# The end of a mixture-of-experts stage, its last block and its pooled sums, and the order of the first loads

## The chip, the cores and the metric

The kernel runs on one core of a Trainium2 chip. TensorE (PE in the profile), VectorE (DVE), ScalarE (ACT), GpSimd (POOL) and SyncE (SP) run their own instruction streams, joined by semaphores. The metric is device time in microseconds; the median of 3 runs is 857.94 (857.0 to 859.44).

## The reference

A macaron block on x of shape (4, 512, 256), float32:

```python
x = x + 0.5 * ffn(layernorm(x))
x = x + attention(layernorm(x))        # lightning attention, 16 heads, chunks of 128
x = x + 0.5 * ffn(layernorm(x))        # the same weights

def ffn(x):                            # 12 experts, top 3
    probs = softmax(x @ Wr + br); top_vals, top_idx = top_k(probs, 3)
    ew = softmax(top_vals); out = 0
    for e in range(12):
        sel = top_idx == e             # tokens that chose e
        w_e = sum(where(sel, ew, 0)) / max(sel.sum(), 1)      # one weight per expert
        h = relu(x @ w1[e] + b1[e]) @ w2[e] + b2[e]           # 256 -> 640 -> 256
        out = out + sel.any(-1) * (w_e * h)
    pooled = out.mean(axis=1)          # one row per batch
    phi = sigmoid(relu(pooled @ Wp1 + bp1) @ Wp2 + bp2)
    return out * (1 - 0.8 * (phi > 0.7))
```

## The kernel before, in words

The program calls the ffn stage twice (f = 0 and 1, "call 0" and "call 1") with attention between. The 2048 tokens are 16 tiles of 128, four chunks of positions (`NC`) by four batches (`B`). Each call has three parts.

*Routing* normalises the tokens, stores them as rows in DRAM (`xn_rows`), computes the router and builds a table that sorts the 6144 token-expert pairs into 35 blocks of 256 (`NB`), each block one expert's.

*Blocks.* For each block POOL gathers its 256 rows by two indirect DMAs, PE transposes them (L816), multiplies by `w1` (`first`, L824: 30 matmuls), ACT applies relu (L695), DVE splits the result into a high and a low half-precision part (L1321, L1323), PE multiplies by `w2` (`second`, L840: 30 matmuls), DVE weighs it and adds b2 (`weigh`, L1331), and POOL adds the rows to an accumulator in DRAM by two indirect DMAs (`scatter`, L510). Even blocks go to accumulator 0, odd ones to accumulator 1 (`LANES`). PE interleaves three blocks: transposes of block b + 2, `first` of b + 1, `second` of b. On POOL gather b + 4 stands ahead of scatter b. In call 0 the weights are split into two half-precision parts for one expert per block in the first dozen blocks (L583, L1112), which lengthens those blocks.

*Combine.* SP waits for all scatters (L470) and loads both accumulators, chunk by chunk, into `O` and `O2` (L474); DVE adds them (L1390); PE sums every batch over its tokens with a column of ones, 32 float matmuls (L905); DVE scales (L1392), PE and ACT compute phi from two small products, DVE turns it into a factor, and updates x by `O` times the factor (L1407). In call 1 SP writes each batch of x out after its update (L480).

All orders are written out by hand; each engine runs its own program, and semaphore waits set the rest. SP issues in program order: inputs, weights, zeros for the two accumulators of call 0 (L429, `clear_sums`), b2 broadcast to all partitions (L465), attention weights and the zeros of call 1 between blocks, accumulators, output. POOL's first scatter of a call waits for the zeros; its first gathers wait for the table. b2 is multiplied by the experts' weights on ACT in call 0 (L681), on POOL in call 1 (L524).

In the profile L759 is the helper through which all matmuls are recorded, so one line stands for many; a float32 matmul is recorded as two instructions.

## Time and profile before

| | us |
|---|---|
| median of 3 runs | 857.94 |
| profiled execution, whole | 856.17 |
| its span, first to last instruction | 854.4 |
| PE busy | 693.0 (81%) |
| DVE busy | 530.5 (62%) |
| POOL busy | 429.3 (50%) |
| ACT busy | 310.4 (36%) |

The span falls into a start of some 60 us, 35 blocks of call 0 until about 340, its combine until about 370, attention until about 515, routing of call 1 until 555, 35 blocks until 815, and the last combine until the end. PE's busy share is near full in the blocks and low in both combines. Busy time counts an engine's instructions; the granted clock of PE, given beside it in the windows, says at which speed they ran (1.00 is 2.4 GHz, 0.50 is 1.2 GHz).

### The profile page before, as it was taken

Reading aid. Unit: us, or ns where it says so; the run is one execution under the profiler, and the core shown is the slowest. Engines: PE = TensorE matmul, PEld = TensorE weight load, DVE = VectorE, ACT = ScalarE, POOL = GpSimd, SP = SyncE. Lnnn points to the kernel's source line nnn. Section 1 sums busy time; section 2 is a strip of 40 time slices with the busy share of each in tenths; the row PEclk is TensorE's granted clock in tenths of the full one; section 3 lists DMA queues with packets and bytes.
Section 4 is the critical chain, followed back from the end, with each engine's and each line's share of the span. In section 5 each row is a group of like instructions: output and inputs, shape, how many; then the busy total and the mean of one; then the engine's idle time right before and its main releaser. Section 6 shows DMA issues by size and latency. Waiting matters only on the chain. (4 is left out here: it accounts for less than half of the span.)

```text
span 854.4 us, 20887 instructions
## 1 busy us (share of the span) xinstructions
PE 693.0 (81%) x6526; PEld 602.8 (71%) x6527; DVE 530.5 (62%) x1066; ACT 310.4 (36%) x692; POOL 429.3 (50%) x304
## 2 busy tenths in 40 slices
PE   1415999899999996659999984169999999999834
PEld 1314777788889985657777773159999999999734
DVE  6894998745555553268888879935555555555413
ACT  3785866433333331023222212323333333333200
POOL 0014488888888875010101000076888888888520
PEclk9756999999999999569999995579999999999965
DMA  9998144655555554610000003033444444444373
GB/s 307 377 365 283 30 72 62 148 93 112 95 111 92 111 93 62 204 49 3 0 0 0 1 2 99 18 112 57 76 77 74 74 75 76 76 74 74 50 196 123
DMA packets 76739, 85.51 MB, mean 100 GB/s; under 512 B 6944, under 2 KB 68384, under 8 KB 76320
## 3 DMA queue, kind: packets, MB, share of 16 engines
q0 software_dynamic: 26880, 36.72, 26.2%
q1 hardware_dynamic: 49824, 48.35, 17.0%
q8 instruction: 19, 0.31, 0.2%
q14 instruction: 16, 0.13, 0.1%
HBM read 50.97 MB, written 34.08 MB: 100 GB/s over the span
## 5 line engine op out<-in xcount | busy, mean ns | idle before, releaser
L759 PE MATMUL PS<-W,A 128*128 (+1 forms) x2228 | 275.1, 279 | 14.1 <-DVE A L1452 7.5
L759 PE MATMUL PS<-A,W 128*128 128x256 f16 (+1 forms) x2356 | 278.5, 277 | 4.3 <-issue 2.8
L510 POOL DMA_INDIRECT expert_sums<-A,place x140 | 233.6, 1668 | 75.0 <-issue 39.3
L495 POOL DMA_INDIRECT A<-xn_rows,token x140 | 177.0, 1265 | 175.4 <-DVE token L1287 125.2
L759 PEld LDWEIGHTS PS<-A,W 128*128 (+1 forms) x2356 | 236.8, 110 | 34.9 <-issue 7.2
L759 PEld LDWEIGHTS PS<-W,A 128*128 128x128 f16 (+1 forms) x2228 | 225.6, 103 | 46.2 <-issue 9.3
L695 ACT ACTIVATE A<-PS,b1s 128x256 f32<-128x256 f32 x350 | 135.5, 478 | 189.5 <-PE PS L759 186.7
L1321 DVE CAST A<-A 128x1280 f16<-128x1280 f32 x70 | 58.6, 838 | 201.6 <-ACT A L695 201.6
L1323 DVE TENSOR_TENSOR A<-A 128x1280 f16<-128x1280 f32 x70 | 104.5, 1492 | 2.4
L759 PE MATMUL PS<-A 32*128 32x128 f32 (+3 forms) x1248 | 67.5, 284 | 30.4 <-DVE A L1264 23.5
L688 ACT ACTIVATE A<-PS 128x512 f16<-128x512 f32 x70 | 42.0, 599 | 117.4 <-PE PS L816 117.4
L759 PEld LDWEIGHTS PS<-A 32*128 32x128 f32 (+3 forms) x1248 | 51.7, 150 | 43.9 <-DVE A L1264 30.3
L554 POOL TENSOR_TENSOR X<-X,W 128x256 f32 x16 | 11.6, 725 | 109.3 <-ACT A L605 103.6
L1331 DVE SCALAR_TENSOR_TENSOR A<-PS,wsc,A 128x256 f32<-128x256 f32 x140 | 60.9, 476 | 7.7 <-PE PS L759 7.7
L816 PE MATMUL PS<-C,A 128*128 128x128 f32 x280 | 44.3, 283 | 24.6 <-DMA A<-xn_rows,token 23.0
L816 PEld LDWEIGHTS PS<-C,A 128*128 128x128 f32 x280 | 33.5, 145 | 28.0 <-DMA A<-xn_rows,token 22.1
L1315 DVE SCALAR_TENSOR_TENSOR A<-PS,A 128x512 f16<-128x512 f32 x70 | 47.7, 682 | 6.6 <-ACT A L688 6.5
L759 PE MATMUL PS<-ones,A 128*128 128x1 f32 x128 | 27.8, 352 | 27.7 <-DVE A L1390 27.7
L759 PEld LDWEIGHTS PS<-ones,A 128*128 128x128 f32 x128 | 27.5, 332 | 28.3 <-DVE A L1390 28.2
L1436 DVE TENSOR_TENSOR A<-PS,A 128x1024 f32<-128x1024 f32 x32 | 39.1, 1222 | 2.1 <-PE PS L759 1.8
L1112 DVE SCALAR_TENSOR_TENSOR W<-W,wscale (+1 forms) x48 | 39.2, 878 | 0.6 <-ACT W L583 0.6
L619 ACT ACTIVATE A<-PS,bqk_s 128x128 f32<-128x128 f32 x64 | 18.3, 369 | 54.8 <-PE PS L759 54.8
(154 smaller groups left out, 417.9 us busy)
## 6 DMA issues: line engine op xcount, KB each, us to landing
W<-w SPq DMA_DIRECT2D x24, 640.0 KB, 11.1
A<-expert_sums SPq DMA_DIRECT2D x16, 512.0 KB, 7.5
expert_sums<-zeros SPq DMA_DIRECT2D x2, 2304.0 KB, 19.9
expert_sums<-zeros SPq DMA_DIRECT2D x12, 384.0 KB, 2.7
xn_rows<-A SPq DMA_DIRECT2D x8, 512.0 KB, 7.1
A<-b SPq DMA_DIRECT2D x2, 1536.0 KB, 10.8
A<-xn_rows,token POOLq DMA_INDIRECT x140
expert_sums<-A,place POOLq DMA_INDIRECT x140, 3.8
```

The lines of the kernel that those rows point to most:

```text
L495: nc.gpsimd.indirect_dma_start(XG[q][:, u * D:(u + 1) * D], None, xn_dram[:, :], bass.IndirectOffsetOnAxis(ap=token[:, at:at + 1], axis=0) ...
L510: nc.gpsimd.indirect_dma_start(sums_dram[f][q][:, :], bass.IndirectOffsetOnAxis(ap=place[:, at:at + 1], axis=0), YO[q][:, u * D:(u + 1) * ...
L688: nc.scalar.mul(XH[q], TB, X_SCALE).then_inc(xh_ready, 1)
L695: ins = nc.scalar.activation(HF[q][:, c * W * P:(c + 1) * W * P], hidden(q, c), ACT.Relu, bias=b1s[:, bass.ds(e * IC + c, 1)], scale=H_SHIFT)
L759: return nc.tensor.matmul(out_, l, r, start=start, stop=stop_, skip_group_check=True)
L816: ins = nc.tensor.transpose(TB[:, k, u * P:(u + 1) * P], XG[q][:, u * D + k * P:u * D + (k + 1) * P], ident)
L1112: v.scalar_tensor_tensor(cut[:, bass.ds(e * (2 * SLOT) + (SLOT + at), SLOT // 2)], raw[:, bass.ds(e * SLOT + (SLOT + at), SLOT // 2)], sca ...
L1315: v.scalar_tensor_tensor(XL[q], TB, X_SCALE, XH[q], ALU.mult, ALU.subtract).then_inc(xl_ready, 1)
L1321: v.tensor_copy(HH[q], HF[q]).then_inc(hh_ready, 1)
L1323: v.tensor_tensor(HL[q], HF[q], HH[q], ALU.subtract).then_inc(hl_ready, 1)
L1331: ins = v.scalar_tensor_tensor(YO[q][:, u * D:(u + 1) * D], bank[7][:, u * D:(u + 1) * D], wsc[:, bass.ds(e, 1)], b2w[:, bass.ds(e * D, D) ...
L1436: v.tensor_tensor(PM[g].rearrange("p r s c -> p r (s c)"), PS[:, 0:4, 0:2 * P], dmask_s[:, g].rearrange("p r s c -> p r (s c)"), ALU.mult) ...
```

## The change

Four edits, in both calls unless said otherwise. First, in SP's program the zeros of call 0 and the b2 loads now wait for the gathers of blocks 0 and 1. Second, in call 1 b2 is multiplied on ACT (12 instructions) instead of on POOL (2). Third, the last block (34) goes through relu, split, second layer and scatter in pieces: hidden chunks (0, 1), (2, 3), (4), and the two halves of 128 tokens one after the other, in two PSUM banks. Fourth, the combine: the four loads of the odd accumulator wait only for its own scatters and for the split of block 34 (`O2` lies elsewhere so that it may), the even ones for theirs; PE sums the two accumulators without waiting for DVE's add, by matmuls whose stationary is a 128x4 matrix with one column of ones and whose moving operand is the 256-column tile, so that the sums are four rows; these are scaled, turned to columns by two transposes and copied. The updates and the output of call 1 go in halves.

On SP, the place between the weight loads and the attention weights at the start of call 0 (`expert_sums<-zeros` is a zero fill, `A<-b` is b2). Before:

```order
L429 DMA expert_sums_0<-zeros 4608x1x128
L429 DMA expert_sums_1<-zeros 4608x1x128
L465 DMA A<-b 128x3072
L445 DMA W<-w_qkvT 128x512
L447 DMA W<-w_qkvT 128x256
```

Now:

```order
L474 DMA A<-b 128x3072
L439 DMA expert_sums_0<-zeros 4608x1x128
L439 DMA expert_sums_1<-zeros 4608x1x128
L455 DMA W<-w_qkvT 128x512
L457 DMA W<-w_qkvT 128x256
```

b2 stands ahead of the fills, and all three behind the wait for the first gathers.

On SP, the end of call 1. Before:

```order
L416 DMA xn_rows<-A 128x4x256 x4
L465 DMA A<-b 128x3072
L474 DMA A<-expert_sums_0 128x4x256
L474 DMA A<-expert_sums_1 128x4x256
L474 DMA A<-expert_sums_0 128x4x256
```

Now:

```order
L426 DMA xn_rows<-A 128x4x256 x4
L474 DMA A<-b 128x3072
L486 DMA A<-expert_sums_1 128x4x256 x4
L486 DMA A<-expert_sums_0 128x4x256 x4
L494 DMA out<-X 128x2x256 x8
```

The odd accumulator comes first as a whole, and the output has eight pieces where it had four.

On PE, the end of call 1, from the last matmuls of block 34 on (`C` holds the identity of the transposes). Before:

```order
L759 MATMUL PS<-W,A 128x256 x2
L759 MATMUL PS<-ones,A 128x1 x32
L759 MATMUL PS<-pooled,Wp_s 128x4 x2
L759 MATMUL PS<-phid,Wp_b 128x4
L113 UNCONDITIONAL_BRANCH
```

Now:

```order
L796 MATMUL PS<-W,A 128x256 x16
L796 MATMUL PS<-A,of_batch 4x256 x32
L972 MATMUL PS<-C,A 128x4 x2
L796 MATMUL PS<-pooled,Wp_s 128x4 x2
L796 MATMUL PS<-phid,Wp_b 128x4
```

The 32 matmuls of one column have become 32 of 256 columns with four rows of result, and two transposes follow.

The diff, cut to its core:

```diff
+        of_batch = sb("of_batch", [P, B, B])
...
-        O2 = A[:, 0:T * D].rearrange("p (i d) -> p i d", i=T)
-        assert T * D <= xn_at
+        O2 = A[:, bufs_at:bufs_at + T * D].rearrange("p (i d) -> p i d", i=T)
+        assert bufs_at + T * D <= xn_at
+        pooled_rows = A[0:B, 0:D]
...
+        TAIL = ((0, 2), (2, 4), (4, IC))
...
-            sp.wait_ge(zeros_ready, 1)
-            for lane in range(LANES):
-                clear_sums(0, lane, 0, 1)
...
 
                 sp.wait_ge(table_psum, f + 1)
+                for q in range(2):
+                    sp.wait_ge(gathered[q], 16 * W * (TURNS[q] * f + 1))
                 sp.dma_start(b2w, b2.rearrange("(a e) h -> a (e h)", a=1).to_broadcast([P, E * D])).then_inc(b2_in, 16)
                 if f == 0:
+                    sp.wait_ge(zeros_ready, 1)
+                    for lane in range(LANES):
+                        clear_sums(0, lane, 0, 1)
                     load_between_blocks()
 
-                for q in range(2):
...
-                    for lane, into in enumerate((O, O2)):
-                        sp.dma_start(into[:, tiles, :], sums_t[f][lane][:, tiles, :]).then_inc(sums_in[c], 16)
+                sp.wait_ge(hl_ready, FREE + NB * (f + 1))
+                for lane, into in ((1, O2), (0, O)):
+                    sp.wait_ge(y_sent[lane], 16 * W * TURNS[lane] * (f + 1))
+                    for c in range(NC):
+                        tiles = slice(c * B, (c + 1) * B)
+                        sp.dma_start(into[:, tiles, :], sums_t[f][lane][:, tiles, :]).then_inc(sums_in[lane][c], 16)
                 if f == 0:
...
-                sp.wait_ge(x_new, 2 * B + b + 1)
-                sp.dma_start(out_t[:, :, b], Xc[:, :, b]).then_inc(x_out, 16)
-            sp.wait_ge(x_out, 16 * B)
+                for half in range(2):
+                    chunks = slice(half * NC // 2, (half + 1) * NC // 2)
+                    sp.wait_ge(x_new, 2 * B + 2 * b + half + 1)
+                    sp.dma_start(out_t[:, chunks, b], Xc[:, chunks, b]).then_inc(x_out, 16)
+            sp.wait_ge(x_out, 32 * B)
 
         def scale_of(e, n):
...
                     pool.sem_inc(pool_held, 1)
-                pool.wait_ge(y_ready, FREE + f * NB + b + 1)
-                pool.sem_inc(pool_held, 1)
+                if b < NB - 1:
+                    pool.wait_ge(y_ready, FREE + f * NB + b + 1)
+                    pool.sem_inc(pool_held, 1)
                 for u in range(W):
+                    if b == NB - 1:
+                        pool.wait_ge(tail_y, W * f + u + 1)
+                        pool.sem_inc(pool_held, 1)
                     at = b * W + u
                     nc.gpsimd.indirect_dma_start(
...
-
-                pool.wait_ge(b2_in, 16 * (f + 1))
-                pool.wait_ge(w_ready, f + 1)
-                v = b2w.rearrange("p (e h) -> p e h", e=E)[:, start:stop_]
-                nc.gpsimd.tensor_tensor(v, v, wexp[:, start:stop_].unsqueeze(2).to_broadcast([P, stop_ - start, D]),
-                                        ALU.mult).then_inc(b2w_ready, 1)
-
             LAG = 4
...
-                    if f == 1 and b >= 2:
-
-                        weigh_b2(1, E // 2 * (b - 2), E // 2 * (b - 1))
                     gather(f, b)
...
+
+                def relu_tail():
+                    b = NB - 1
+                    e = act.value_load(eob[0:1, b:b + 1], min_val=0, max_val=E - 1)
+                    act.wait_ge(hl_ready, f * NB + b + 1)
+                    for p, (start, stop_) in enumerate(TAIL):
+                        act.wait_ge(tail_first, len(TAIL) * f + p + 1)
+                        for c in range(start, stop_):
+                            ins = nc.scalar.activation(HF[0][:, c * W * P:(c + 1) * W * P], hidden(0, c),
+                                                       ACT.Relu, bias=b1s[:, bass.ds(e * IC + c, 1)],
+                                                       scale=H_SHIFT)
+                        ins.then_inc(tail_relu, 1)
+                    act.wait_ge(tail_relu, len(TAIL) * (f + 1))
...
                     first_plain = PREP
+                else:
+                    high(1, 1)
+                    relu(0, 0)
+                    high(2, 0)
+                    act.wait_ge(b2_in, 32)
+                    act.wait_ge(w_ready, 2)
+                    for half in range(2):
+                        for m in range(E // 2 * half, E // 2 * (half + 1)):
+                            weighted_b2(m)
+                        if half == 0:
+                            relu(1, 1)
...
 
...
                                 n += 1
-                    ins.then_inc(layer1, 1)
+                        if tail and c + 1 in (TAIL[0][1], TAIL[1][1], TAIL[2][1]):
+                            ins.then_inc(tail_first, 1)
+                    if tail:
+                        pe.wait_ge(tail_first, len(TAIL) * (f + 1))
+                        pe.sem_inc(layer1, 1)
+                    else:
+                        ins.then_inc(layer1, 1)
 
                 def second(b, q):
...
+                def second_tail():
+                    b = NB - 1
+                    e = pe.value_load(eob[0:1, b:b + 1], min_val=0, max_val=E - 1)
+                    pe.wait_ge(y_ready, f * NB + b + 2)
+                    for u in range(W):
+                        n = 0
+                        for c in range(IC):
+                            if u == 0 and c % 2 == 0:
+                                pe.wait_ge(tail_low, len(TAIL) * f + c // 2 + 1)
+                            for part, src in ((0, HH), (0, HL), (1, HH)):
+                                w = w2h[:, bass.ds(e * (2 * SLOT) + (part * SLOT + c * D), D)]
+                                ins = matmul(tail_result(u), src[0][:, (c * W + u) * P:(c * W + u + 1) * P], w,
+                                             n == 0, n == 14)
+                                n += 1
+                        ins.then_inc(tail_second, 1)
+                    pe.wait_ge(tail_second, W * (f + 1))
+                    pe.sem_inc(layer2, 1)
...
+                first(NB - 1, 0, tail=True)
                 second(NB - 2, 1)
-                second(NB - 1, 0)
+                second_tail()
 
...
-                    for k in range(KC):
+                if f == 0:
+                    pe.wait_ge(ones_ready, B)
+                for lane, sums in ((1, O2), (0, O)):
+                    for c in range(NC):
+                        pe.wait_ge(sums_in[lane][c], 16 * (f + 1))
                         for b in range(B):
-                            col = k * B + b
-                            ins = matmul(bank[1][:, col:col + 1], O[:, c * B + b, k * P:(k + 1) * P],
-                                         ones[:, 0:1], c == 0 and col == 0, c == NC - 1)
-                ins.then_inc(pool_psum, 1)
+                            ins = matmul(bank[1][0:B, 0:D], of_batch[:, b, :], sums[:, c * B + b, :],
+                                         lane == 1 and c == 0 and b == 0, lane == 0 and c == NC - 1 and b == B - 1)
+                        ins.then_inc(pool_psum, 1)
+                pe.wait_ge(pool_turned, 2 * f + 1)
+                for k in range(KC):
+                    ins = nc.tensor.transpose(bank[4][:, k * B:(k + 1) * B], pooled_rows[:, k * P:(k + 1) * P],
+                                              ident[0:B, 0:B])
+                ins.then_inc(pool_turned, 1)
...
+                v.memset(of_batch[:, :, :], 0.0).then_inc(zeros_ready, 1)
+                dve.wait_ge(zeros_ready, 3)
+                for b in range(B):
+                    v.memset(of_batch[:, b, b:b + 1], 1.0).then_inc(ones_ready, 1)
...
+                def split_tail():
+                    dve.wait_ge(layer2, f * NB + NB - 1 + 1)
+                    for p, (start, stop_) in enumerate(TAIL):
+                        cols = slice(start * W * P, stop_ * W * P)
+                        dve.wait_ge(tail_relu, len(TAIL) * f + p + 1)
+                        v.tensor_copy(HH[0][:, cols], HF[0][:, cols]).then_inc(tail_high, 1)
+                        dve.wait_ge(tail_high, len(TAIL) * f + p + 1)
+                        v.tensor_tensor(HL[0][:, cols], HF[0][:, cols], HH[0][:, cols],
+                                        ALU.subtract).then_inc(tail_low, 1)
+                    dve.wait_ge(tail_low, len(TAIL) * (f + 1))
+                    dve.sem_inc(hh_ready, 1)
+                    dve.sem_inc(hl_ready, 1)
+
+                def weigh_tail():
+                    b = NB - 1
+                    e = dve.value_load(eob[0:1, b:b + 1], min_val=0, max_val=E - 1)
+                    dve.wait_ge(y_sent[0], sent(f, b, 0))
+                    for u in range(W):
+                        dve.wait_ge(tail_second, W * f + u + 1)
+                        v.scalar_tensor_tensor(YO[0][:, u * D:(u + 1) * D], tail_result(u), wsc[:, bass.ds(e, 1)],
+                                               b2w[:, bass.ds(e * D, D)], ALU.mult, ALU.add).then_inc(tail_y, 1)
+                    dve.wait_ge(tail_y, W * (f + 1))
+                    dve.sem_inc(y_ready, 1)
+
...
+                split_tail()
                 weigh(NB - 2, 1)
-                weigh(NB - 1, 0)
+                weigh_tail()
 
             def sent(f, b, q):
 
...
-                    dve.wait_ge(sums_in[c], 16 * LANES * (f + 1))
-                    v.tensor_tensor(Oc[:, c], Oc[:, c], O2c[:, c], ALU.add).then_inc(chunks_added, 1)
-                dve.wait_ge(pool_psum, f + 1)
-                v.tensor_scalar(pooled[:, :], bank[1][:, 0:KC * B], 1.0 / N, None, ALU.mult).then_inc(pool_ready, 1)
+                    for lane in range(LANES):
+                        dve.wait_ge(sums_in[lane][c], 16 * (f + 1))
+                    dve.wait_ge(pool_psum, 2 * NC * f + NC + c + 1)
+                    v.tensor_tensor(Oc[:, c], Oc[:, c], O2c[:, c], ALU.add)
+                v.tensor_scalar(pooled_rows[:, :], bank[1][0:B, 0:D], 1.0 / N, None, ALU.mult).then_inc(pool_turned, 1)
+                dve.wait_ge(pool_turned, 2 * f + 2)
+                v.tensor_copy(pooled[:, :], bank[4][:, 0:KC * B]).then_inc(pool_ready, 1)
...
+                    for b in range(B):
+                        for half in range(2):
+                            update(slice(half * NC // 2, (half + 1) * NC // 2), b)
 
             def attention():
```

## Rows read from the trace of the kernel before

**Rows 1.** Chain of waits, end of call 1: start us, us, what.
```profile
810.38 3.46 PE PS L759 x30
...
817.50 3.80 DMA expert_sums<-A,place
...
821.73 4.68 DMA A<-expert_sums
...
845.07 4.87 DVE X L1407 x4
```

**Rows 2.** Timeline, call 1's end: start, us, engine line op, [idle before].
```profile
810.91 1.55 POOL L510 DMA_INDIRECT expert_sums<-A,place  x1 [3.00 <-DVE A L1331]
...
821.32 7.47 SPq L474 DMA_DIRECT2D A<-expert_sums  x8
...
827.71 13.98 PE L759 MATMUL PS<-ones,A 128*128 128x1 f32 x64 [13.89 <-DVE A L1390]
...
835.41 1.23 DVE L1390 TENSOR_TENSOR A<-A 128x1024 f32<-128x1024 f32 x1 [1.45 <-DMA A<-expert_sums]
```

**Rows 3.** Timeline, end of call 0, PE on the pooled sums.
```profile
350.18 13.81 PE L759 MATMUL PS<-ones,A 128*128 128x1 f32 x64 [13.77 <-DVE A L1390]
```

**Rows 4.** Timeline, first attention tiles, float matmuls on PE.
```profile
373.60 3.40 PE L759 MATMUL PS<-A,W 128*128 128x128 f32 x16 [0.46 <-ACT A L612]
...
379.20 1.03 PE L759 MATMUL PS<-W,A 128*128 128x256 f32 x4
```

**Rows 5.** Windows: stretch, length, busy by engine, PE clock, DMA share, GB/s.
```profile
78.00:82.00 4.00, 4.00 (x32) 3.35 (x31) 2.16 (x3) 3.97 (x9) 0.79 (x2) 0.81 0.42 159
374.00:378.00 4.00, 2.99 (x16) 2.80 (x15) 2.05 (x5) 0.97 (x4) 1.43 (x2) 0.69 0.00 0
...
815.00:819.00 4.00, 0.00 (x0) 0.00 (x0) 0.00 (x0) 0.00 (x0) 3.05 (x2) 0.72 0.51 62
...
835.00:839.00 4.00, 4.00 (x21) 4.00 (x20) 1.23 (x1) 0.00 (x0) 0.00 (x0) 0.50 0.00 0
```

**Rows 6.** Timeline, start of call 0: gathers on POOL, first transposes on PE.
```profile
63.41 1.16 POOL L495 DMA_INDIRECT A<-xn_rows,token  x1 [0.30 <-issue]
...
66.43 0.95 POOL L495 DMA_INDIRECT A<-xn_rows,token  x1 [0.30 <-issue]
...
69.12 1.11 PE L816 MATMUL PS<-C,A 128*128 128x128 f32 x4 [11.07 <-DMA A<-xn_rows,token]
...
73.86 1.12 PE L816 MATMUL PS<-C,A 128*128 128x128 f32 x4 [2.98 <-DMA A<-xn_rows,token]
```

**Rows 7.** DMA issues of the page: count, KB each, median us to landing.
```profile
expert_sums<-zeros SPq DMA_DIRECT2D x2, 2304.0 KB, 19.9
...
A<-b SPq DMA_DIRECT2D x2, 1536.0 KB, 10.8
```

**Rows 8.** Windows, start of call 0.
```profile
62.00:66.00 4.00, 0.00 (x0) 0.00 (x0) 3.96 (x6) 1.42 (x3) 3.39 (x3) 0.50 1.15 349
```

**Rows 9.** Timeline, start of call 1: gather on POOL, transposes on PE.
```profile
557.23 0.98 POOL L495 DMA_INDIRECT A<-xn_rows,token  x1 [0.30 <-issue]
...
560.52 1.12 PE L816 MATMUL PS<-C,A 128*128 128x128 f32 x4 [7.18 <-DMA A<-xn_rows,token]
...
563.95 1.08 PE L816 MATMUL PS<-C,A 128*128 128x128 f32 x4 [1.68 <-DVE A L1315]
```

**Rows 10.** Timeline, call 0, first scatters and the stretch behind them.
```profile
95.31 1.61 POOL L510 DMA_INDIRECT expert_sums<-A,place  x1 [10.97 <-DVE A L1331]
...
99.40 0.49 ACT L681 ACTIVATE A<-A,wexp  x1
...
99.93 2.04 POOL L495 DMA_INDIRECT A<-xn_rows,token  x1 [0.30 <-issue]
...
121.26 0.65 PE L816 MATMUL PS<-C,A 128*128 128x128 f32 x4 [0.35 <-DMA A<-xn_rows,token]
```

**Rows 11.** Timeline, routing of call 0 on DVE.
```profile
39.67 0.35 DVE L1208 TENSOR_REDUCE A<-A 128x16 f32<-128x192 f32 x1 [1.36 <-ACT A L659]
```

38 lines of the change are left out of this document (21 added, 17 removed).

## The prediction

> **What bounds the kernel now.** I read the chain of waits first, from its end. The last 50 us are one serial chain [rows 1]: second-layer matmuls of the last block (34) at 810.38, its scatters landing at 821.3, accumulators landing at 826.4, pooled sums on PE, gate, update at 845.07, output. The timeline of that stretch [rows 2] tells why it is long: SP starts all eight accumulator loads together at 821.32, after the last scatter, and PE then takes 13.98 us for 64 instructions on the pooled sums, from 827.71 to 841.69. Call 0 ends the same way: 13.81 us [rows 3]. The other places the change touches are the starts of the two calls, where PE waits for gathers [rows 6, 9]. Between them a block takes PE some 7 us and nothing changes.
>
> **Ends of both calls: what moves.** The odd accumulator (blocks 1, 3, ... 33) is complete once block 33's second scatter has landed. That scatter is issued at 810.91 + 1.55 + 0.30 = 812.8 and needs the 3.80 of [rows 1]: 816.6. Before, SP waited for block 34 as well. Now SP needs only block 33's scatters, and block 33 is weighed a little earlier, since the pieces of block 34 no longer occupy DVE as one lump; the drain that PE waits for after the first layer gives some of it back. I take 816.2 and SP's 0.35. A chunk of one accumulator is half of what took 4.68 [rows 1]; between 2.3 and 4.7 I take 3.6. PE starts on pooled sums at 820.1 instead of 827.7.
>
> The sums are computed another way. Before: 32 float matmuls, each two instructions, with a full 128x128 stationary and one moving column, 13.98 / 64 = 0.22 us each. Now: 32 matmuls, 64 instructions, with a 4-column stationary and 256 moving columns. That form is not in the trace; the nearest rows are attention's [rows 4]. At half clock 16 instructions of 128 columns took 3.40, so 0.425 for 256 columns and 27.2 for 64. At full clock four of 256 columns took 1.03, 0.26 each with the last one's drain in it, so 0.23 in a stream (estimate), 14.7 to 16.5 for 64. So the clock decides. PE's clock has fallen to 0.50 before the loads arrive: it is 0.72 on average in 815 to 819, PE idle since 813.8 [rows 5]. It starts cold. In attention the float stream from 373.60 lifted it: 0.69 in 374 to 378 means full speed from about 376.5, 2.9 us after the start; in call 0 it rose at about 79.5, 5.6 us after PE became busy at 73.86 [rows 5, 6]. I take 4 us: 9.4 instructions cold, 54.6 at 0.23 = 12.6, end at 820.1 + 4 + 12.6 = 836.7. Chunks arrive faster than PE takes them (eight within 14 us of 821.3 before [rows 2]), so only the first is waited for.
>
> The Trainium skill (TensorE: Matmul & The Clock Gate, LDWEIGHTS) says that loading a stationary takes time by its columns, not its rows; four columns would be almost free. Then 256 columns in two passes at 2.4 GHz give 0.213 an instruction by the page's rule (estimate), PE's end 0.9 us earlier in each call, and a time of 847.8. No row has a four-column stationary, so the sum stays with 0.23.
>
> Behind PE's end there is now more. DVE's last chunk add (1.23 [rows 2]) was hidden under PE before; now it waits for PE's last chunk and stands between PE and the gate. Then an eviction of four rows (a 256-element operation, a third of the add, 0.4), two transposes (half of the 1.1 of four [rows 6], 0.5), and a copy in place of the one that was there: with handoffs 2.2 us, bounds 1.8 to 2.8. So the end of each call: -5.0 + 2.2 = -2.8. Bounds: clock full from the start -4.7; never full +7.8 (rival A).
>
> The last block in pieces lets even-lane scatters start about 1.5 us earlier, by POOL's spacing of 1.85 for four of them. That is hidden: PE is still on odd chunks, until about 829. It costs if the even chunks came later than PE reaches them; they have several us.
>
> The output now goes in eight halves of 4 x 1.22 [rows 1]: the first half leaves about 0.6 earlier, eight fixed costs instead of four come back as a little DVE time. I take -0.3 in call 1 (bounds -0.6 to +0.5).
>
> **Start of call 0.** SP's two zero fills (2 x 2304 KB) and b2 (1536 KB) [rows 7] were ahead of the first gathers; at 62 to 66 the DMA engines are saturated at 349 GB/s [rows 8]. Block 0's gather ended issue at 64.57 and PE got it at 69.12, 4.5 later; block 1's at 67.38 and 73.86, 6.5 later [rows 6]. In call 1, with b2 alone in flight, it is 2.3 [rows 9]. Without either I take 1.9: transposes of block 0 at 66.5 (-2.6); those of block 1 follow 3.4 us after the first ones where no data is waited for [rows 9], at 69.9 instead of 73.86: -3.9.
>
> Not all of it is kept. The fills now begin after block 1's gather lands, 69.3. With b2 and two gathers they are 6.8 MB, at 349 GB/s 19.5 us: the zeros are down at about 90. POOL waits for them before gather 4, which stands ahead of scatter 0 on its queue. Gather 4 takes 2.3 to 4.4 us (0.95 to 2.04 an issue [rows 6, 10]), so scatter 0 starts at about 93.2; before it was 95.31 [rows 10]. From there POOL runs without pause, 0.30 between issues, and PE waits for its gathers (0.35 at 121.26) [rows 10]: POOL sets the pace until the weights are prepared. So what is kept is POOL's gain, -2.0. Bounds: -3.9 (fills land before 88) to +8 (rival B).
>
> **Start of call 1.** b2 is issued only after two gathers: block 0's lands in 1.9 instead of 2.3: -0.4. The two POOL multiplications become twelve on ACT, 0.49 each [rows 10]: six before the second relu delay it by some 0.5 us, six delay the next copy, both ahead of PE's need by a whole first layer (3.4 us). If b2 landed 3 us later than I think, that cover is gone and the same 3 us come back.
>
> **Setup.** One memset, a wait and four tiny memsets on DVE, below 0.7 us: DVE waits 1.36 for ACT at 39.67 [rows 11], which swallows it.
>
> **Sum.** -2.8 - 2.8 - 0.3 - 2.0 - 0.4 = -8.3 us. The profiled execution took 856.17: 847.9. The median of the runs shown is 1.77 above it: 849.6.
>
> **Rivals.**
> A, slower: the clock does not rise under the new stream. For: the old pooled sums kept PE's row full for 14 us and the clock stayed at 0.50 (835 to 839 [rows 5]); the new ones use 4 of 128 columns. Against: old instructions moved one column, the new ones move 256, like the attention stream that did lift it. All 64 at 0.425: end at 847.3, the gate 847.3 + 2.2 - 841.69 = 7.8 later in each call, 15.6 - 2.7 = +12.9: 870.8. It decides from about 10 us at half clock on: 23.5 instructions cold, 40.5 at 0.23, end at 839.4, all gain gone. Chance 0.12.
>
> B: b2 and the fills land one after the other as slowly as before, 10.8 and 19.9 us from issue [rows 7]: zeros down at 69.5 + 30.7 = 100.2, scatter 0 at 103.3, +8 instead of -2: 859.6. For: each fill writes runs of 512 bytes. Against: those times hold the wait behind other traffic, and at 349 GB/s the fills were most of it. Chance 0.08.
>
> C: the odd loads delay block 34's scatter. The row that shows it is gather 1, 6.5 us under heavy load against 2.3 [rows 6, 9]. A slip of 4.2 moves the even chunks to about 824 to 832, still ahead of PE; above 6.7 it counts one for one. At a slip of 10 in each call: 856.2. Chance 0.04. The Trainium skill (DMA: Bandwidth & Descriptors, Issuing engines are not separate DMA queues) speaks for it: transfers of SP and POOL run on the same 16 engines and interleave. By that rule some slip is certain; the rows say it stays hidden.
>
> D: more than forecast: clock up at once and fills early: -4.7 x 2 - 0.3 - 3.9 - 0.4 = -14.0: 843.9. Chance 0.1.
>
> **How the numbers follow.** Forecast 849.6 with 0.66. Range 843 to 859: D below, and above a clock that rises only after 10 us with fills that are late, short of B; left out are A, B and little else. A measurement tells a change from none at 0.3%, 2.6 us: 855.4 and 860.5. Faster: nearly all of the forecast's 0.66, D and a little of C: 0.76. Same: most of B and C: 0.10. Slower: A and what is worse than B: 0.14.
>
> **What would show it.** Odd accumulator loads at about 816.5 and pooled sums from about 820 (less the earlier gains); 64 instructions that start near 0.42 and go to 0.21 to 0.26; a chunk add, an eviction and two transposes behind the last of them; gate about 2.8 earlier. Transposes of block 0 at 66.5, zeros landing near 90, scatter 0 at 93. It is wrong if the clock row reads 0.50 throughout the pooled sums, if scatter 0 starts after 95.3, or if PE waits for even chunks.

## The result and the profile after

The changed kernel takes 852.47 us (median of 11 runs, 848.82 to 855.04), the kernel before in the same job 857.57 (11 runs, 855.06 to 860.25): ratio 0.9944, 95% interval 0.9926 to 0.9963, so 5 us faster. The forecast was 849.6, its range 843 to 859. The profiled execution took 852.16, with a span of 850.4 against 854.4.

The end of call 1, timeline of the changed kernel (start, us, engine line operation, idle before and what ended it):

```profile
799.82 3.44 PE L796 MATMUL PS<-A,W 128*128 128x256 f16 x30
...
815.11 1.54 POOL L528 DMA_INDIRECT expert_sums<-A,place  x1 [0.30 <-issue]
815.20 9.39 SPq L486 DMA_DIRECT2D A<-expert_sums  x8
...
819.73 16.84 PE L796 MATMUL PS<-A,of_batch 128*4 128x256 f32 x64 [7.36 <-DMA A<-expert_sums]
836.71 1.23 DVE L1487 TENSOR_TENSOR A<-A 128x1024 f32<-128x1024 f32 x1 [0.50 <-PE PS L796]
...
838.85 0.72 PE L796 MATMUL PS<-pooled,Wp_s 128*128 128x4 f32 x4 [0.26 <-DVE pooled L1490]
841.67 5.39 DVE L1504 SCALAR_TENSOR_TENSOR X<-A,gate,X 128x512 f32<-128x512 f32 x8
```

SP loads from 815.20, while POOL is still issuing block 34's last scatter at 815.11; before, it was 821.32 [rows 2]. The even loads follow only once that scatter has landed:

```profile
822.58 2.01 SPq L486 DMA_DIRECT2D A<-expert_sums  x4
```

PE sums from 819.73 instead of 827.71, but its 64 instructions take 16.84 instead of 13.98, and behind them stand an add, an eviction, two transposes and a copy: 2.28 from PE's end (836.57) to the first small product, where it was 0.26 (841.69 to 841.95). PE's speed in that stream, windows (length, busy by engine, PE clock, DMA share, GB/s):

```profile
815.00:819.00 4.00, 0.00 (x0) 0.00 (x0) 0.00 (x0) 0.00 (x0) 1.54 (x1) 0.54 0.79 168
819.00:823.00 4.00, 3.27 (x8) 0.99 (x9) 0.00 (x0) 0.00 (x0) 0.00 (x0) 0.50 1.09 331
823.00:827.00 4.00, 4.00 (x14) 1.38 (x13) 0.00 (x0) 0.00 (x0) 0.00 (x0) 0.68 0.99 330
827.00:831.00 4.00, 4.00 (x20) 1.57 (x18) 0.00 (x0) 0.00 (x0) 0.00 (x0) 1.00 0.87 286
```

Half speed until about 825.6, then full: 8 instructions in the window at 0.50, 20 in the one at 1.00. The clock did rise, unlike in the kernel before, where it stayed at 0.50 through the pooled sums [rows 5].

The starts, timeline. Call 0, then call 1:

```profile
66.42 1.12 PE L853 MATMUL PS<-C,A 128*128 128x128 f32 x4 [8.29 <-DMA A<-xn_rows,token]
69.39 0.34 SPq L474 DMA_DIRECT2D A<-b  x1
69.78 12.32 SPq L439 DMA_DIRECT2D expert_sums<-zeros  x2
69.85 1.08 PE L853 MATMUL PS<-C,A 128*128 128x128 f32 x4 [1.67 <-DVE A L1386]
...
93.14 0.98 POOL L509 DMA_INDIRECT A<-xn_rows,token  x1 [18.60 <-DMA expert_sums<-zeros]
96.75 1.89 POOL L528 DMA_INDIRECT expert_sums<-A,place  x1 [0.30 <-issue]
98.30 0.95 PE L853 MATMUL PS<-C,A 128*128 128x128 f32 x4 [3.99 <-DMA A<-xn_rows,token]
...
557.32 1.11 PE L853 MATMUL PS<-C,A 128*128 128x128 f32 x4 [6.68 <-DMA A<-xn_rows,token]
559.81 0.35 SPq L474 DMA_DIRECT2D A<-b  x1
561.63 5.65 PE L796 MATMUL PS<-A,W 128*128 128x256 f16 x30
568.39 0.66 PE L853 MATMUL PS<-C,A 128*128 128x128 f32 x4 [1.11 <-DMA A<-xn_rows,token]
```

In call 0 the first transposes come at 66.42 and 69.85 instead of 69.12 and 73.86 [rows 6]; POOL stands 18.60 before gather 4, scatter 0 comes at 96.75 instead of 95.31 [rows 10], and PE waits 3.99 for that gather. In call 1 PE starts earlier, runs the first layer of block 0 in 5.65 instead of 4.78, and then waits 1.11 instead of 0.32 for the gather of block 2, which is issued as b2 is. The same place in the kernel before:

```profile
564.84 4.78 PE L759 MATMUL PS<-A,W 128*128 128x256 f16 x30
...
569.94 0.66 PE L816 MATMUL PS<-C,A 128*128 128x128 f32 x4 [0.32 <-DMA A<-xn_rows,token]
```

Cut at five points, the two traces give (34 is the first layer of block 34, gate the first update of x):

| stretch | before | changed | difference |
|---|---|---|---|
| start to 34, call 0 | 323.95 | 323.16 | -0.8 |
| 34 to gate, call 0 | 43.42 | 41.18 | -2.2 |
| gate to gather 0 of call 1 | 188.09 | 188.42 | +0.3 |
| gather 0 to 34, call 1 | 245.91 | 247.06 | +1.2 |
| 34 to gate, call 1 | 43.70 | 41.85 | -1.9 |
| gate to end | 9.33 | 8.73 | -0.6 |

So the ends won 4.7, the two stretches with the starts together gave 0.4 back, and the stretch between, which no edit touched, 0.3. One trace is thin ground for parts of 1 us, so twelve more kernels were run, each in five rounds against the kernel before. A to E are lengths in the one trace of each: A start to 34 of call 0; B from there to the first small product behind the pooled sums; C on to gather 0 of call 1 (attention and routing, the same code everywhere); D gather 0 to 34 of call 1; E as B, in call 1.

| kernel | median | ratio to before (95%) | A | B | C | D | E |
|---|---|---|---|---|---|---|---|
| before | | | 323.95 | 40.30 | 191.21 | 245.91 | 40.58 |
| changed | 852.47 | 0.9944 (0.9926-0.9963) | 323.16 | 38.67 | 190.93 | 247.06 | 39.03 |
| 1 new ends only | 851.52 | 0.9950 (0.9926-0.9975) | 323.96 | 39.50 | 191.59 | 246.38 | 37.64 |
| 2 new starts only | 859.59 | 1.0032 (1.0009-1.0055) | 322.21 | 41.12 | 193.21 | 247.22 | 40.39 |
| 3 wait at scatter | 852.77 | 0.9953 (0.9926-0.9979) | 321.92 | 38.80 | 194.35 | 247.63 | 39.12 |
| 4 warm PE | 848.38 | 0.9919 (0.9887-0.9952) | 324.75 | 37.83 | 193.00 | 246.27 | 37.00 |
| 5 add behind | 850.36 | 0.9909 (0.9878-0.9940) | 322.36 | 38.57 | 190.74 | 247.74 | 37.13 |
| 6 b2 first | 852.65 | 0.9935 (0.9913-0.9957) | 323.00 | 37.43 | 191.03 | 246.34 | 39.34 |
| 7 = 4 + 5 + 6 | 845.77 | 0.9852 (0.9824-0.9881) | 323.51 | 36.18 | 190.98 | 246.58 | 35.87 |
| 8 = 1 + 4 + 5 | 846.75 | 0.9856 (0.9826-0.9886) | 323.30 | 36.30 | 192.45 | 246.38 | 39.31 |
| 9 = 7, sum once | 852.72 | 0.9936 (0.9912-0.9960) | 324.38 | 40.00 | 190.83 | 246.12 | 38.27 |
| 10 = 7, b2 on POOL | 848.18 | 0.9891 (0.9871-0.9911) | 324.16 | 36.26 | 190.87 | 247.23 | 36.28 |
| 11 block 34 whole | 850.87 | 0.9921 (0.9898-0.9944) | 323.03 | 38.04 | 191.65 | 247.09 | 38.75 |
| 12 = 7, block whole | 846.96 | 0.9880 (0.9847-0.9912) | 324.18 | 37.08 | 190.70 | 245.88 | 36.23 |

C says how much a single trace can be trusted: the same code took 190.7 to 194.4.

### The profile page after: what moved, and what is told of

It reads as the page before. It is cut to its first block, busy times and chain, and to the rows that moved or that the text cites. A ratio compares the mean times of both kernels' runs of the same rounds, so it can differ in the third digit from the quotient of the medians.

```text
span 850.4 us, 20944 instructions
## 1 busy us (share of the span) xinstructions
PE 700.3 (82%) x6530; PEld 588.5 (69%) x6531; DVE 532.6 (63%) x1085; ACT 315.0 (37%) x704; POOL 422.0 (50%) x302
## 4 chain that ended last, share of the span: by engine, by line
PE 66%; DVE 9%; DMA 8%; issue 7%; POOL 4%; SPq 3%; ACT 1%; DVEq 0%; ACTq 0%; POOLq 0%
PE PS L796 62%; PE PS L853 3%; POOL expert_sums L528 3%; DMA expert_sums<-zeros 3%; DMA expert_sums<-A,place 2%; POOL A L509 2%; DVE A L1335 2%; DMA W<-w 1%; SPq L432 1%; DMA A<-expert_sums 1%; DMA A<-xn_rows,token 1%; DVE A L1332 1%; DVE A L1555 1%; DVE A L1246 1%; DVE X L1504 1%
## 5 line engine op out<-in xcount | busy, mean ns | idle before, releaser
L528 POOL DMA_INDIRECT expert_sums<-A,place x140 | 231.2, 1651 | 65.2 <-issue 40.4
L706 ACT ACTIVATE A<-PS,b1s 128x256 f32<-128x256 f32 x340 | 131.3, 478 | 179.3 <-PE PS L796 177.6
L1392 DVE CAST A<-A 128x1280 f16<-128x1280 f32 x68 | 56.2, 827 | 197.6 <-ACT A L706 197.5
L1394 DVE TENSOR_TENSOR A<-A 128x1280 f16<-128x1280 f32 x68 | 101.5, 1492 | 2.3
L1402 DVE SCALAR_TENSOR_TENSOR A<-PS,wsc,A 128x256 f32<-128x256 f32 x136 | 59.1, 476 | 5.0 <-PE PS L796 5.0
L796 PE MATMUL PS<-A,of_batch 128*4 128x256 f32 x128 | 32.8, 424 | 15.2 <-DMA A<-expert_sums 15.2
L796 PEld LDWEIGHTS PS<-A,of_batch 128*4 128x4 f32 x128 | 11.9, 94 | 35.7 <-issue 15.1
```

Of the source, the lines that this page charges most:

```text
L528: nc.gpsimd.indirect_dma_start(sums_dram[f][q][:, :], bass.IndirectOffsetOnAxis(ap=place[:, at:at + 1], axis=0), YO[q][:, u * D:(u + 1) * ...
L706: ins = nc.scalar.activation(HF[q][:, c * W * P:(c + 1) * W * P], hidden(q, c), ACT.Relu, bias=b1s[:, bass.ds(e * IC + c, 1)], scale=H_SHIFT)
L796: return nc.tensor.matmul(out_, l, r, start=start, stop=stop_, skip_group_check=True)
L1392: v.tensor_copy(HH[q], HF[q]).then_inc(hh_ready, 1)
L1394: v.tensor_tensor(HL[q], HF[q], HH[q], ALU.subtract).then_inc(hl_ready, 1)
L1402: ins = v.scalar_tensor_tensor(YO[q][:, u * D:(u + 1) * D], bank[7][:, u * D:(u + 1) * D], wsc[:, bass.ds(e, 1)], b2w[:, bass.ds(e * D, D) ...
```

## Experiments

**1. New ends only.** The old order of SP's loads; b2's multiplication on ACT stays.

```diff
+            sp.wait_ge(zeros_ready, 1)
+            for lane in range(LANES):
+                clear_sums(0, lane, 0, 1)
             for f in calls:
...
-                for q in range(2):
-                    sp.wait_ge(gathered[q], 16 * W * (TURNS[q] * f + 1))
...
                 if f == 0:
-                    sp.wait_ge(zeros_ready, 1)
-                    for lane in range(LANES):
-                        clear_sums(0, lane, 0, 1)
```

> The changed kernel with the old order of loads at both starts: SP issues the zeros of call 0 and b2 where it did before, with no wait for the first gathers. The last block in pieces, the combine and b2's multiplication on ACT in call 1 stay. Theory of the traces (T): the new ends are worth -2.2 and -2.4 us (update of each call and the output), the new starts together lost about 0.7, so this kernel is 0 to 1.5 us FASTER than the changed one, about 5 us below before: ratio to before 0.993 to 0.995. Theory of the forecast's ledger (F): the starts were worth -2.4, so this kernel is 2.4 us slower than the changed one, 2.7 below before: ratio 0.997. In the trace T expects transposes of block 0 of call 0 again at 69.1, and gathers 2 in call 1 that PE does not wait 1.1 for.

Measured: 0.9950, all of the change's gain within the interval; 0.997 is inside it too, so this run alone does not refute the forecast's ledger. In the trace block 0's transposes of call 0 come at 69.29 again and PE does not wait for gather 2 of call 1, as T expected.

**2. New starts only.** The kernel before with those waits and b2 on ACT in call 1.

```diff
                 sp.wait_ge(table_psum, f + 1)
+                for q in range(2):
+                    sp.wait_ge(gathered[q], 16 * W * (TURNS[q] * f + 1))
...
                 if f == 0:
+                    sp.wait_ge(zeros_ready, 1)
+                    for lane in range(LANES):
+                        clear_sums(0, lane, 0, 1)
```

> The kernel before with the other half alone: the zeros of call 0 and b2 behind the gathers of blocks 0 and 1, and b2 multiplied on ACT in call 1. Ends as before. T: call 0's start gains about 1 us by its end, call 1's start gives back about 1.5 (gather 2 lands behind b2, and first-layer matmuls run longer at half clock since they begin earlier): ratio 0.999 to 1.002. F: -2.0 and -0.4, ratio 0.997. Scatter 0 of call 0 at about 96.7 in both.

Measured: 1.0032, interval above 1 and far from 0.997: the starts alone lose. F falls. T had the sign; its bound 1.002 is inside the interval, the middle is worse. Its one trace does not show where the loss sits: A is 1.7 shorter than before and D 1.3 longer, -0.4 together, while B and C, in which nothing was changed, are 0.8 and 2.0 longer. In this trace b2 is issued at 563.55, and PE waits for block 2's gather and runs its first layer longer:

```profile
563.55 0.35 SPq L464 DMA_DIRECT2D A<-b  x1
565.48 5.14 PE L770 MATMUL PS<-A,W 128*128 128x256 f16 x30
572.31 0.66 PE L827 MATMUL PS<-C,A 128*128 128x128 f32 x4 [1.70 <-DMA A<-xn_rows,token]
```

**3. The wait for the zeros behind gather 4.**

```diff
-                pool.wait_ge(sums_cleared[f], 16 * LANES * (1, CLEARS)[f])
                 for b in range(NB):
                     if b + LAG < NB:
                         gather(f, b + LAG)
+                    if b == 0:
+                        pool.wait_ge(sums_cleared[f], 16 * LANES * (1, CLEARS)[f])
                     scatter(f, b)
```

> The changed kernel with POOL's wait for the zeros moved from ahead of gather 4 to behind it, right ahead of scatter 0. Theory P (the wait of POOL for the zeros at 93, and PE's 3.99 us for gather 4 behind it, is a real loss): gather 4 is issued at about 75 to 80, PE's wait at block 4 goes, PE does not fall to half clock there, and 2 to 4 us of the span go. Theory Q (the blocks up to some dozen are paced by the preparation of the weights on ACT and DVE, so PE catches up whatever happens at block 4): PE's wait at block 4 goes but the time from block 12 on is the same within 0.5 us.

```profile
94.16 2.98 POOL L528 DMA_INDIRECT expert_sums<-A,place  x1 [12.15 <-DMA expert_sums<-zeros]
94.27 0.60 PE L854 MATMUL PS<-C,A 128*128 128x128 f32 x4
...
103.78 0.66 PE L854 MATMUL PS<-C,A 128*128 128x128 f32 x4 [1.42 <-DMA A<-xn_rows,token]
```

PE no longer waits at block 4; it waits 1.42 at block 5 instead, whose gather stands behind scatter 0 on POOL. Scatter 0 comes 2.6 earlier, the first layer of block 12 is 1.5 earlier than in the changed kernel (so Q's 0.5 isn't met either), and A is 321.92, the lowest of all, 1.2 below the changed kernel; kernels with one and the same start differ by twice that (322.21 to 324.75). The median shows no gain: 0.9953 against 0.9944. P's 2 to 4 us are not there; a gain of about 1 stays open.

**4. PE kept busy ahead of the pooled sums.**

```diff
+                for _ in range(60):
+                    matmul(bank[5][:, 0:D], w1h[:, 0:P], w1h[:, 0:D], True, True)
                 for lane, sums in ((1, O2), (0, O)):
```

> The changed kernel with 60 half-precision matmuls of 256 columns (no use, constant operands, a bank that is free) on PE ahead of the pooled sums of each call, to keep PE busy while it would wait for the odd accumulator. Theory K (the pooled sums begin at half clock because PE was idle before them, which costs some 14 instructions at 0.425 instead of 0.216): the granted clock is 1.00 when they begin, 64 instructions take 13.8 us instead of 16.0 and 16.8, and each call ends 2.2 to 2.9 us earlier: 4 to 5.5 us below the changed kernel. Theory L (the half speed of the first ones is the form's own or data arriving, not the clock): no change of the pooled sums, 0 us. A third outcome: the dummies themselves run at half clock and end after the odd chunks have landed, so that they delay the sums: 0 to 3 us slower.

```profile
814.56 6.71 PE L796 MATMUL PS<-W 128*128 128x256 f16 x60
...
821.95 3.83 PE L796 MATMUL PS<-A,of_batch 128*4 128x256 f32 x16 [0.68 <-DMA A<-expert_sums]
...
826.05 10.52 PE L796 MATMUL PS<-A,of_batch 128*4 128x256 f32 x48 [0.28 <-DMA A<-expert_sums]
```

```profile
815.00:819.00 4.00, 4.00 (x39) 3.60 (x37) 0.00 (x0) 0.00 (x0) 3.09 (x2) 1.00 0.71 79
819.00:823.00 4.00, 3.32 (x26) 2.23 (x25) 0.00 (x0) 0.00 (x0) 0.00 (x0) 1.00 0.91 278
```

K holds for the mechanism: the clock is 1.00 when the sums begin, and from the first to the last they take 14.62 instead of 16.84. Its size is less than expected: 0.9919 is 2.2 us below the changed kernel (intervals overlap). In call 0 PE now waits 1.48 us for a chunk.

**5. The last add behind the copy.**

```diff
-                    v.tensor_tensor(Oc[:, c], Oc[:, c], O2c[:, c], ALU.add)
+                    if c < NC - 1:
+                        v.tensor_tensor(Oc[:, c], Oc[:, c], O2c[:, c], ALU.add)
...
                 v.tensor_copy(pooled[:, :], bank[4][:, 0:KC * B]).then_inc(pool_ready, 1)
+                v.tensor_tensor(Oc[:, NC - 1], Oc[:, NC - 1], O2c[:, NC - 1], ALU.add)
```

> The changed kernel with DVE's add of the last chunk moved from ahead of the pooled row's scaling to behind the copy to the pooled columns, in both calls. Theory S (the add, 1.22 us in call 0 and 1.23 in call 1, stands in the serial chain between PE's last sum and the gate): each call's gate comes 1.2 earlier, the add runs while PE and ACT compute phi (2.8 us from the first small product to the update), total -2.4: ratio to before 0.991 to 0.992 where the changed kernel has 0.994. Theory U (DVE would be late for the first update, or the add stays ahead of something else): 0 to -1.

```profile
836.32 0.17 DVE L1491 COPY pooled<-PS 128x8 f32<-128x8 f32 x1 [0.37 <-PE PS L972]
836.40 1.22 DVE L1492 TENSOR_TENSOR A<-A 128x1024 f32<-128x1024 f32 x1
838.22 0.17 DVE L1495 TENSOR_SCALAR gate<-gate 128x4 f32<-128x4 f32 x1 [0.60 <-ACT gate L780]
```

S holds: from PE's last sum to the first small product 1.16 instead of 2.28 in call 1, 1.16 instead of 2.27 in call 0, and DVE is free again before ACT has the gate. 0.9909, as S said.

**6. b2 of call 1 not behind the gathers.**

```diff
-                for q in range(2):
-                    sp.wait_ge(gathered[q], 16 * W * (TURNS[q] * f + 1))
+                if f == 0:
+                    for q in range(2):
+                        sp.wait_ge(gathered[q], 16 * W)
```

> The changed kernel with b2 of call 1 not waiting for the gathers of blocks 0 and 1 (in call 0 it still does). Theory G (b2 that is issued just behind gather 1 delays the gather of block 2: PE waited 1.11 us for it, and what remains is the phase of the clock's rise): block 0's transposes come 0.4 to 0.5 later after their gather, the wait for block 2's gather goes, and from gather 0 to the first layer of block 34 it takes 246.4 as in the kernel with the old starts, against 247.1: -0.7. In the median -0.7 or less, which five rounds may not show. Theory H (the order of b2 does not matter, only the multiplication on ACT does): that stretch stays at 247.1 and the second layer of block 0 still waits.

D is 246.34, as G said, and the wait for block 2's gather is gone; the median (0.9935) can't show 0.7. Over all traces: with b2 behind the gathers (the changed kernel, 2, 3, 4, 5, 11) D is 247.2 in the mean, with b2 ahead (the other eight) 246.35; the two groups overlap, since 4 (246.27) lies among the eight and 10 (247.23) among the six. The gather itself does gain from the change: from gather 0's issue to the first transposes 4.53 to 4.63 in the six, 5.06 to 6.16 in the eight. More is lost behind it: in the six PE waits 0.25 to 2.31 for gather 2, and not at all in the six of the eight that multiply on ACT.

**7. Four, five and six together.** The three edits above, nothing else.

> The changed kernel with 60 half-precision matmuls that keep PE busy ahead of the pooled sums, the last chunk's add behind the copy, and b2 of call 1 not waiting. If the three gains add: -3.1 (the matmuls, by the medians of the first runs), -2.4, -0.7 = -6.2 against the changed kernel: ratio to before 0.987. If warm sums are already bound by the landing of the accumulators (1.48 us of waiting for the second odd chunk in call 0), the add still gains its 1.2 per call: not less than -5.

```profile
812.59 8.85 SPq L487 DMA_DIRECT2D A<-expert_sums  x8
...
817.64 1.89 PE L797 MATMUL PS<-A,of_batch 128*4 128x256 f32 x8 [0.97 <-DMA A<-expert_sums]
819.72 12.25 PE L797 MATMUL PS<-A,of_batch 128*4 128x256 f32 x56 [0.18 <-DMA A<-expert_sums]
```

845.77, ratio 0.9852 (0.9824 to 0.9881): faster than both kernels, the changed one's interval lies wholly above. B and E are 36.18 and 35.87, 4.1 and 4.7 below the kernel before: PE waits 0.97 for the first chunk and 0.18 for the second, and runs through. The span is 6.1 below the changed kernel's (844.3 against 850.4), as the sum of the three gains had said (-6.2).

**8. The same ends, all starts old.** Experiment 1 with the edits of 4 and 5.

> The kernel with the new ends and the old starts, with the 60 matmuls and the last add behind the copy. Against the previous kernel it differs only in the start of call 0 (zeros and b2 ahead of the gathers). If the new start of call 0 is worth nothing by the time the weights are prepared (theory T: between -1.7 and +0.8 in single traces), the two are the same within 1 us; if the forecast's -2.0 is right after all, this one is 2 us slower. Ratio to before 0.987 to 0.990.

0.9856: the same as 7 within 1 us (A 323.30 against 323.51), so the new start of call 0 is worth nothing that can be measured; the two intervals are too wide for the medians alone to exclude 2 us. Its trace holds an accident that shows K again: the second odd chunk came late, PE stood 2.12, and the clock fell in spite of the warm matmuls.

```profile
818.65 1.89 PE L794 MATMUL PS<-A,of_batch 128*4 128x256 f32 x8 [0.79 <-DMA A<-expert_sums]
...
822.65 13.94 PE L794 MATMUL PS<-A,of_batch 128*4 128x256 f32 x56 [2.12 <-DMA A<-expert_sums]
```

```profile
823.00:827.00 4.00, 4.00 (x13) 1.28 (x11) 0.00 (x0) 0.00 (x0) 0.00 (x0) 0.59 1.08 352
```

E is 39.31 there, 3.4 more than in 7: 1.9 more of waiting, and 1.7 by which the 56 instructions behind it are slower (13.94 against 12.25).

**9. One sum over added chunks.** Version 7 with 110 warm matmuls, and:

```diff
-                for lane, sums in ((1, O2), (0, O)):
-                    for c in range(NC):
-                        pe.wait_ge(sums_in[lane][c], 16 * (f + 1))
+                for c in range(NC):
+                    pe.wait_ge(chunks_added, NC * f + c + 1)
...
```

> The version with warm matmuls, the last add behind the copy and b2 of call 1 not waiting, but with the pooled sums taken once, over the accumulators that DVE has added (as in the kernel before), in row form: 32 instructions instead of 64, each chunk behind DVE's add; 110 warm matmuls instead of 60, since PE's sums start later. In the version that it is compared with, PE's 64 warm instructions bound the end: 13.8 us from the first odd chunk, 817.64 to 831.97, while the DMA share falls at about 827.5. Theory M (the separate sums of both accumulators are the bound once warm): the last chunk lands at about 827.5, its add ends at 828.9, its 8 instructions at 830.6, so each call ends 1.3 earlier, less 0 to 1 of handoffs: -1 to -2.5 in all, ratio to before 0.982 to 0.984. Theory N (what ends last is the chain of the accumulators anyway, and the add stands in it again): 0 to +2, ratio 0.985 to 0.988.

```profile
814.04 12.17 PE L798 MATMUL PS<-W 128*128 128x256 f16 x110
817.88 7.72 SPq L488 DMA_DIRECT2D A<-expert_sums  x8
828.52 1.23 DVE L1489 TENSOR_TENSOR A<-A 128x1024 f32<-128x1024 f32 x1 [14.11 <-DMA A<-expert_sums]
...
829.80 8.76 PE L798 MATMUL PS<-A,of_batch 128*4 128x256 f32 x32 [3.59 <-DVE A L1489]
832.97 1.23 DVE L1489 TENSOR_TENSOR A<-A 128x1024 f32<-128x1024 f32 x1 [0.22 <-DMA A<-expert_sums]
```

M falls: 0.9936, some 7 us more than version 7. The first even chunk lands 10.6 after SP's first issue, the last 15.1; the 110 matmuls end 3.6 too early and the 32 sums start at half speed (the clock is 0.57 in the window 830 to 832; 0.27 each in the mean). Here half of PE's work behind the landing costs more than all of it in the landing's shadow. With more warm matmuls it might come near 7; that wasn't tried.

**10. b2 on POOL again,** on version 7: the two multiplications of the kernel before in place of the twelve on ACT.

```diff
+                    if f == 1 and b >= 2:
+                        weigh_b2(1, E // 2 * (b - 2), E // 2 * (b - 1))
                     gather(f, b)
...
```

> The same version with call 1's b2 multiplied on POOL again, as in the kernel before, so that the start of call 1 is the old one altogether. In the traces so far the stretch from gather 0 of call 1 to the first layer of block 34 took 245.9 us with the multiplication on POOL (one trace), 246.3 to 246.6 on ACT (four traces with b2 not waiting). Theory V (the multiplication on ACT costs 0.4 to 0.6): that stretch is 245.9 again, the median 0.4 lower, which rounds of this number don't show: it is read in the trace. Theory W (the 0.5 is the phase of the clock): 246.3 to 246.6.

D is 247.23, neither V's 245.9 nor W's 246.3 to 246.6. V falls: the 245.91 of the kernel before was a lucky trace, not the price of POOL (block 0's transposes came 5.06 behind gather 0 there and 6.16 here, PE's wait for gather 2 is 0.32 there and 0.90 here). 0.9891 is if anything worse than 7. ACT's twelve cost nothing visible.

**11. Block 34 whole,** on the changed kernel; **12.** the same on version 7.

```diff
-                first(NB - 1, 0, tail=True)
+                first(NB - 1, 0)
                 second(NB - 2, 1)
-                second_tail()
+                second(NB - 1, 0)
```

(relu, split, weigh and scatter likewise.)

> The changed kernel with the last block whole, as in the kernel before: one relu, split, second layer and scatter; the combine, the loads and the starts stay. The forecast: the pieces let the even scatters start 1.5 earlier, hidden behind PE's odd sums, and the odd loads 0.4 earlier: undone, each call is 0 to 0.5 later, total 0 to +1. Rival (the pieces matter, since the last block's second layer starts 1.1 later when whole, PE goes cold later and the even chunks are then the late ones): +1.5 to +3 in all, PE waiting for even chunks. Rival (the pieces cost: the drain of 1.04 in front of second(33) goes): -1 in all. Shown by the start of SP's loads, the start of the pooled sums less the start of the first layer of block 34 (19.9 us in call 1), and waits between the 64 instructions.

> The fastest version so far (warm matmuls, last add behind the copy, b2 of call 1 not waiting) with the last block whole instead of in pieces. Theory X (the pieces are hidden, and the drain in front of block 33's second layer costs what block 33 gains): within 1 us of that version, ratio 0.984 to 0.987. Theory Y (the pieces cost, as the first such run hinted with a ratio of 0.9921 against 0.9944): -1.5, ratio 0.983. Theory Z (with warm sums the even chunks become the late ones, and the pieces' 1.5 us counts): +1 to +3, ratio 0.986 to 0.989, with PE waiting among its 64 instructions for an even chunk.

11's end of call 1:

```profile
815.05 10.09 SPq L486 DMA_DIRECT2D A<-expert_sums  x8
...
819.53 16.75 PE L792 MATMUL PS<-A,of_batch 128*4 128x256 f32 x64 [7.27 <-DMA A<-expert_sums]
```

SP loads as early without the pieces, 15.24 behind the first layer of block 34 against 15.38, and PE waits for no even chunk. 0.9921 on the changed kernel, 0.9880 on version 7, once lower and once higher, and both times the intervals overlap: the pieces are worth nothing that these runs show. In 12 the end of call 1 runs through, but in call 0 PE waits for an even chunk (and before it 1.55 for the second odd one):

```profile
356.48 3.62 PE L793 MATMUL PS<-A,of_batch 128*4 128x256 f32 x16 [0.44 <-DMA A<-expert_sums]
```

So Y is not confirmed, and X and Z are not told apart: 0.9880 lies above X's range and in Z's, the interval reaches into both, and Z's wait is there in one call of two.

## Why the prediction was right, point by point, and where it was not

*Odd loads ahead of block 34's scatter: right, 1.2 late.* SP started 0.5 later behind the block's first layer than I had put it, and the first chunk landed 4.5 after the issue instead of 3.9. The 0.4 that I gave for the pieces isn't there (11): what block 33 gains on DVE, the drain ahead of its second layer takes. Rival C's slip came, and stayed hidden: from the issue of block 34's last scatter (815.11) to the even loads that wait for it (822.58) it took 7.5, where the scatter had landed after 3.8 before [rows 1], and PE waited for no even chunk.

*The clock decides the stream: right, the sizes off.* I had 4 us at half speed; it was 5.9 in call 1, 4.1 in call 0, and 2.6 to 6.0 over the twelve streams of all traces that began cold. I had 0.23 an instruction at full speed; 48 took 10.52 in experiment 4, 0.219. In call 1 the errors cancel by luck: PE ended at 836.57, forecast 836.7. But 1.6 of that had been won earlier in the program; behind block 34's first layer PE ended 3.6 earlier, not 5.0. By the rule of the Trainium skill (TensorE: Matmul & The Clock Gate, LDWEIGHTS), that a stationary's loading time goes by its columns, I had estimated 0.213 for a stationary of four; the trace is nearer to it than to my 0.23. Rival A is refuted by the window at 1.00, rival D by the one at 0.50; experiments 4 and 8 show from both sides what idle time of PE ahead of the sums or among them costs by the clock: 2.2 and 1.7 us.

*The tail behind PE: right.* 2.28 against 0.26, +2.0 where I had +2.2. Experiment 5 shows that 1.1 of it was not needed: the add had no reader before the update.

*The last block in pieces, hidden: right* in the changed kernel (11); 12 leaves it open for sums at full clock. *Output in halves:* -0.6, the bound, not -0.3.

*Ends together:* -2.2 and -1.9 in the trace, with the output -4.7; forecast -5.9.

*Start of call 0: the step that failed.* Transposes at 66.42 and 69.85 came as forecast (66.5, 69.9). Scatter 0 did not: forecast 93.2, it came at 96.75, 1.4 later than before and not 2.1 earlier (the text had named a start after 95.3 as what would show it wrong). Of the 3.5, 3.1 lie ahead of gather 4: the zeros landed at 92.3 instead of about 90, and POOL took up gather 4 at 93.14. The gain at PE went at that place too: block 2's first layer began 3.8 earlier than before (87.48 against 91.30), block 3's, behind PE's 3.99 of waiting for gather 4, 0.5 later (99.39 against 98.91).

That POOL sets the pace from there was right. From scatter 0 to scatter 12 it issues one DMA after the other and waits 0.3 between them, in the changed kernel and, but for one wait of 0.74 in 10, in all other traces:

```profile
POOL expert_sums L528 <- issue: 7.6, 25, 0.3
POOL A L509 <- issue: 6.7, 22, 0.3
POOL A L509 <- DMA expert_sums<-A,place: 0.6, 2, 0.3
```

(who waited for whom on POOL from 97 to 187, changed kernel: us in total, times, longest). But I took its run for equally long, so that scatter 0's gain would be kept one to one. Scatter 12, before and now:

```profile
188.02 1.62 POOL L510 DMA_INDIRECT expert_sums<-A,place  x1 [0.30 <-issue]
```

```profile
186.90 1.61 POOL L528 DMA_INDIRECT expert_sums<-A,place  x1 [0.30 <-issue]
```

The run took 90.1 instead of 92.7, which turns 1.4 late into 1.1 early, and block 12's first layer is 1.1 early as well (169.41 against 170.52). In between PE waits three times for a gather (136.35, 152.31, 168.21; 0.4 to 0.8). Behind block 12 the blocks follow each other at PE's 7.0 us, and block 34 began 0.8 earlier. With the old start the run took 92.1 to 92.7 in three traces, with the new one 89.8 to 92.3 in eleven; why its DMAs are issued in less time in some was not settled. Over the traces, the new start is worth -0.3 in A (323.7 in three with the old order, 323.5 in ten with the new, 3 apart), not -2.0, and neither 3 nor 8 against 7 moved the median. Rival B did not come: zeros at 92.3, not 100.2.

*Start of call 1: wrong in sign.* -0.4 forecast, +1.2 in the trace, where all of it is there by the first layer of block 1, and +0.8 over the traces. I counted b2 out of the way of gathers 0 and 1 (worth 1.0, more than I said) and did not count what it is moved in front of: gather 2 is issued at 559.22 and 560.48, b2 at 559.81 between its two halves, and PE has its rows at 568.39, 7.0 us after the second issue ended; gather 0 took 1.8. PE's wait for gather 2 is 0.8 longer than before. That is the rule cited for rival C (the Trainium skill, DMA: Bandwidth & Descriptors, Issuing engines are not separate DMA queues); the trace agrees with it here too, at a place where I had not looked. Nor did I count that the first layer of block 0, which begins earlier, runs longer at half clock (by the granted clock 4.5 us of it, before 2.8): 5.65 instead of 4.78, another 0.9. ACT's twelve multiplications were hidden, as forecast (10).

*Sum.* -8.3 forecast; -4.0 in the trace, -5.1 in the medians. Of the 4.3 that are missing, 1.2 are in the ends and 2.8 in the starts; the rest is the stretch between, which nothing touched. What stays open: experiment 2 puts both starts at +0.8 to +4.7, the changed kernel against experiment 1 at nothing (0.9944 and 0.9950), experiments 7 and 8 that of call 0 alone at nothing; the traces' +0.5 for both lies below the first and agrees with the others.

## What to carry to other kernels

When a load is moved, list what it is moved in front of as well as what it is moved out of the way of: here the second cost more than the first gained. An early start is worth what reaches the engine that sets the pace, here POOL's queue in the first dozen blocks. A serial end is won by starting work in the shadow of a transfer, even twice as much of it, and by keeping TensorE busy up to it; what nothing behind it reads goes behind the result, not ahead. And parts of 1 us are read from several traces: stretches that no edit touched differed by 3.7 us.

## What the runs showed of the hardware

The stretch of attention differs by when the clock rises. From the first small product of call 0 to gather 0 of call 1 it took 190.7 to 194.4 us. Between the changed kernel and experiment 3 all of the difference is there when the first attention tile is through (19.0 and 22.4 us): the window of 376 to 380 reads 1.00 in the one and 0.50 in the other.

The granted clock of a window is not always to be trusted. In the changed kernel every window up to 74 reads 1.00, that of 62 to 66 too, where the kernel before reads 0.50 [rows 8]. The first layer at 70.94 ran 5.23 us, where the same 30 matmuls take 3.44 later; its matmuls start 0.21 apart until 74.5 and 0.11 apart from there on. So these first windows say nothing of the clock:

```profile
70.00:74.00 4.00, 3.99 (x19) 2.72 (x19) 1.84 (x3) 3.03 (x4) 2.50 (x3) 1.00 0.90 276
```

```profile
70.94 5.23 PE L796 MATMUL PS<-A,W 128*128 128x256 f16 x30
```
